# Turning 17 of 52 gathered fields on VectorE, with two marks and two pair blocks moved, in a DLRM tower on one core

## The reference

```
e = stack([tbl_f[ids[:, f]] for f in 26 fields])          # 512 x 26 x 128
sd = einsum('bfd,bd->bf', e, dense)
ss = einsum('bfd,bgd->bfg', e, e);  pairs = ss[:, iu, ju]  # 325 pairs
z = concatenate([dense, sd, pairs], 1);  h = concatenate([z, dense], 1)
h = maximum(h @ W_top1 + b_top1, 0)    # 607 -> 512
h = maximum(h @ W_top2 + b_top2, 0)    # 512 -> 256
y = h @ W_top3                         # 256 -> 1
```

## Time and profile before

| | us |
|---|---|
| median of 3 runs (lowest to highest) | 117.57 (117.4 to 118.24) |
| the profiled execution's own time | 117.33 |
| its span, first to last instruction | 115.3 |
| TensorE matmuls busy | 107.0 |
| VectorE busy | 62.2 |
| ScalarE busy | 62.1 |
| GpSimd busy | 58.3 |

### The profile page before, as it was taken

How to read it: one execution, slowest core, us unless ns; L and a number is a source line. 1 busy time by engine, 2 the same in 40 slices (tenths; PEclk the granted TensorE clock), 3 DMA queues, 4 the chain that set the end, 5 groups by cost and what they waited for, 6 DMA issues and landing times.

```text
span 115.3 us, 3393 instructions
## 1 busy us (share of the span) xinstructions
PE 107.0 (93%) x1514; PEld 86.8 (75%) x1514; DVE 62.2 (54%) x90; ACT 62.1 (54%) x82; POOL 58.3 (51%) x56
## 2 busy tenths in 40 slices
PE   5979899999999999999999998889999987999991
PEld 4637677868888888888887666768787875989891
DVE  0378998689897799798950007107131026008321
ACT  2379999993999999998930405003121016102220
POOL 0177788777777777788777506006677000000000
PEclk9999999999999999999999999999999999999999
DMA  1897976755766975999312201100212100000000
GB/s 41 248 299 276 287 281 227 244 137 200 275 179 218 347 205 144 374 276 336 84 46 51 67 1 28 28 6 23 50 47 68 28 6 0 6 0 6 6 0 1
DMA packets 6416, 14.84 MB, mean 129 GB/s; under 512 B 2125, under 2 KB 2637, under 8 KB 6402
## 3 DMA queue, kind: packets, MB, share of 16 engines
q1 hardware_dynamic: 4306, 10.94, 28.7%
q0 software_dynamic: 1664, 3.41, 10.7%
q10 hardware_dynamic: 432, 0.27, 0.8%
HBM read 14.62 MB, written 0.00 MB: 127 GB/s over the span
## 4 chain that ended last, share of the span: by engine, by line
PE 66%; ACT 13%; issue 9%; DVE 6%; DMA 4%; ACTq 1%
PE gram_ps L533 11%; PE h_ps L505 9%; PE h_ps L501 8%; PE gram_ps L501 7%; PE gram_ps L505 7%; ACT dist L294 5%; PE h_ps L557 5%; DMA raw<-oh 4%; PE h_ps L550 3%; PE h_ps L580 3%; ACT hi L282 3%; PE h_ps L567 3%; PE turn_ps L521 2%; ACT onehot L297 2%; DVE zfull L431 2%
## 5 line engine op out<-in xcount | busy, mean ns | idle before, releaser
L260 POOL DMA_INDIRECT got<-tbl,ids_sb x52 | 58.1, 1117 | 31.0 <-issue 14.9
L416 DVE TENSOR_SCALAR onehot<-ids_bc,rows_sb 128x1024 fp32r<-128x1024 int16 (+1 forms) x47 | 31.0, 718 | 5.4 <-DMA rows_sb<-rows 3.7
L418 DVE TENSOR_TENSOR lo<-raw,hi 128x1024 fp32r<-128x1024 f32 (+2 forms) x14 | 17.1, 1224 | 4.2 <-ACT hi L282 3.6
L501 PE MATMUL h_ps<-onehot,hi 128*128 128x512 f32 x60 | 16.7, 412 | 1.0 <-ACT onehot L297 0.8
L533 PE MATMUL gram_ps<-vecs 128*27 128x27 f32 x1024 | 13.3, 192 | 2.2 <-issue 1.5
L533 PEld LDWEIGHTS gram_ps<-vecs 128*27 128x27 f32 x1024 | 10.6, 104 | 6.3 <-issue 4.1
L308 ACT ACTIVATE vecs<-turn_ps 128x512 f32<-128x512 f32 (+2 forms) x16 | 8.2, 521 | 12.6 <-PE turn_ps L521 12.6
L505 PE MATMUL h_ps<-onehot,lo 128*128 128x512 f32 x60 | 15.0, 390 | 0.0
L501 PEld LDWEIGHTS h_ps<-onehot,hi 128*128 128x128 f32 x60 | 11.0, 192 | 5.1 <-ACT onehot L297 1.9
L431 DVE STREAM_TRANSPOSE zfull<-gram_ps 128x864 f32<-128x864 f32 x3 | 3.2, 1083 | 21.4 <-PE gram_ps L533 21.4
L297 ACT ACTIVATE onehot<-dist,rows_sb 128x1024 fp32r<-128x1024 f32 (+1 forms) x13 | 14.1, 1087 | 0.4
(11 more groups left out here) (55 smaller groups left out, 87.4 us busy)
## 6 DMA issues: line engine op xcount, KB each, us to landing
raw<-oh SPq DMA_DIRECT2D x8, 512.0 KB, 3.7
raw<-oh SPq DMA_DIRECT2D x4, 640.0 KB, 4.1
ids_bc<-ids_oh SPq DMA_DIRECT2D x6, 256.0 KB, 4.3
got<-tbl,ids_sb POOLq DMA_INDIRECT x52, 3.5
w1p_sb<-w_pairs SPq DMA_DIRECT2D x1, 702.0 KB
w1d_sb<-w_dense SPq DMA_DIRECT2D x1, 512.0 KB
w_sb<-w SPq DMA_DIRECT2D x1, 512.0 KB
raw<-oh ACTq DMA_DIRECT2D x2, 128.0 KB, 4.4
```

Source lines behind the costliest of these rows:

```text
L260: nc.gpsimd.indirect_dma_start(out=got[:, t, k, :], out_offset=None, in_=tables[k], in_offset=bass.IndirectOffsetOnAxis(ap=ids_sb[:, at:at ...
L416: nc.vector.tensor_scalar(there, row_numbers, rows_sb[:, c:c + 1], None, ALU.is_equal).then_inc(oh_dve, 1)
L418: nc.vector.tensor_tensor(lo[:, u % 2, 0:width(u)], raw[:, u % RAWS, 0:width(u)], hi[:, u % 2, 0:width(u)], ALU.subtract).then_inc(lo_read ...
L501: nc.tensor.matmul(banks[:, s, :], hi[:, u % 2, q * DIM:(q + 1) * DIM], onehot[:, u % 2, q * BATCH:(q + 1) * BATCH], start=(c == 0), stop= ...
```

## The change

Four edits, all of them of order and of which engine does what:

- Groups (2, 1), (2, 2), (2, 3), (3, 0) and (3, 1) are turned by VectorE. A group becomes 16 instructions of 32 partitions (a block of 32 samples by 32 dimensions for each field of the group), straight from `got` to `vecs`, with a semaphore on the last. TensorE's turns and ScalarE's moves of these groups go, and the banks of the others are counted anew (`BY_PE`). `gram` waits for both kinds. On VectorE the groups stand: (2, 1) and (2, 2) before the pair products of tile 0, (2, 3) between the zt copy of tile 0 and pair products 1, (3, 0) between the zt copy of tile 1 and `relu_h1b(0)`, (3, 1) between `relu_h2_far(0)` and pair products 2.
- In units 0 and 1 ScalarE marks nothing; VectorE marks all four columns.
- In TensorE's order the second and third pair blocks of tile 0 stand behind gram 1, the fourth behind the turn of the pairs of tile 1; one filler is added behind gram 0 in place of a turned group, and three go between gram 1 and layer 1 of tile 1.
- The last layer block takes its two banks in the other order.

```diff
+BY_DVE = [(2, 1), (2, 2), (2, 3), (3, 0), (3, 1)]
+BY_PE = [(t, i) for t in range(TILES) for i in range(GROUPS) if (t, i) not in BY_DVE]
+PE_GROUPS = [sum(u <= t for u, _ in BY_PE) for t in range(TILES)]
+DVE_GROUPS = [sum(u <= t for u, _ in BY_DVE) for t in range(TILES)]
...
-ACT_MARKS = [1, 1, 1, 1, 1, 1, 0, 1, 1, 1, 1, 1, 1, 1]
+ACT_MARKS = [0, 0, 1, 1, 1, 1, 0, 1, 1, 1, 1, 1, 1, 1]
...
-        banks_of = [h1_ps, h1_ps, turn_ps[1:3]]
+        banks_of = [h1_ps, h1_ps, [turn_ps[2], turn_ps[1]]]
...
             move_group(2, 0)
-            move_group(2, 1)
             near_pairs(0)
-            move_group(2, 2)
             near_pairs(1)
-            move_group(2, 3)
             relu_h1a(0)
             relu_h2(0)
-            move_group(3, 0)
             near_pairs(2)
-            move_group(3, 1)
             move_group(3, 2)
...
+            def turn_group(t, i):
+                dve.wait_ge(gathered[t][i], 16 * GROUP[i])
+                for r in range(QUADS):
+                    for c in range(QUADS):
+                        last = nc.vector.transpose(
+                            vecs[BLK * c:BLK * (c + 1), t * P + BLK * r:t * P + BLK * (r + 1),
+                                 GROUP_SLOT[i]:GROUP_SLOT[i] + GROUP[i]].rearrange("d b s -> d s b"),
+                            got[BLK * r:BLK * (r + 1), t, GROUP_AT[i]:GROUP_AT[i + 1], BLK * c:BLK * (c + 1)])
+                last.then_inc(dve_turned, 1)
...
+            turn_group(2, 1)
+            turn_group(2, 2)
             pair_products(0)
             zt_copy(0)
+            turn_group(2, 3)
             pair_products(1)
             zt_copy(1)
+            turn_group(3, 0)
             relu_h1b(0)
             relu_h2_far(0)
+            turn_group(3, 1)
             pair_products(2)
...
-                    pe.wait_ge(vecs_moved, GROUPS * t + GROUPS)
+                    pe.wait_ge(vecs_moved, PE_GROUPS[t])
+                    if DVE_GROUPS[t] > 0:
+                        pe.wait_ge(dve_turned, DVE_GROUPS[t])
...
             gram(0, 6, PARTS)
-            turn_group(2, 1)
             gram(0, 7, PARTS)
             layer1_dense(0, [3])
-            turn_group(2, 2)
-            keep_busy(2, 2 * GROUPS + 1)
+            keep_busy(2, PE_GROUPS[2])
+            keep_busy(2, PE_GROUPS[2])
...
             gram(1, 5, PARTS)
+            gram(1, 6, PARTS)
+            gram(1, 7, PARTS)
             layer1_pairs_of_tile(0, [1])
-            gram(1, 6, PARTS)
             layer1_pairs_of_tile(0, [2])
-            gram(1, 7, PARTS)
+            turn_pairs(1)
             layer1_pairs_of_tile(0, [3])
-            turn_group(2, 3)
-            keep_busy(0, 2 * GROUPS + 2)
-            keep_busy(0, 2 * GROUPS + 2)
-            turn_pairs(1)
-            keep_busy(0, 2 * GROUPS + 2)
             layer1_pairs_of_tile(1)
...
             gram(2, 7, PARTS)
-            turn_group(3, 0)
-            turn_group(3, 1)
             turn_group(3, 2)
+            turn_group(3, 3)
             turn_pairs(2)
-            turn_group(3, 3)
-            pe.wait_ge(vecs_moved, GROUPS * (TILES - 1) + 2)
             layer1_dense(2, [0])
```

More of the change, by code:

```diff
@@ L186, in dlrm_tower @@
         vecs_moved = sem("vecs_moved")
+        dve_turned = sem("dve_turned")
         gram_done = sem("gram_done")
@@ L306, in move_group @@
             def move_group(t, i):
-                act.wait_ge(turned, GROUPS * t + i + 1)
+                n = BY_PE.index((t, i))
+                act.wait_ge(turned, n + 1)
                 nc.scalar.activation(
                     vecs[:, t * P:(t + 1) * P, GROUP_SLOT[i]:GROUP_SLOT[i] + GROUP[i]],
-                    turn_ps[(GROUPS * t + i) % TURN_BANKS][:, 0:GROUP[i] * P].rearrange("d (s b) -> d b s", s=GROUP[i]),
+                    turn_ps[n % TURN_BANKS][:, 0:GROUP[i] * P].rearrange("d (s b) -> d b s", s=GROUP[i]),
                     ACT.Copy).then_inc(vecs_moved, 1)
@@ L515, in turn_group @@
             def turn_group(t, i):
-                n = GROUPS * t + i
+                n = BY_PE.index((t, i))
                 pe.wait_ge(gathered[t][i], 16 * GROUP[i])
```

## The result

The changed kernel took 125.06 us (median, 124.64 to 126.54), the kernel before 117.91: a ratio of 1.060, interval 1.053 to 1.067. It is 7.1 us slower, where 2.3 us faster was forecast. The profiled execution took 124.64, its span is 122.6 us.

What follows compares the result with a forecast made beforehand. TensorE was taken as the bound wherever fed. Gains of 1.1 and 0.59 us and the reorder, less VectorE's delays, ended layer 2 2.1 us earlier: 117.33 to 115.2, written 115.3; range 113.9 to 117.8.

Steps and rivals of the forecast that it cites:

- Head: Look-up part: moving two marks from ScalarE to VectorE starts everything behind it 1.1 us earlier, bounds 0 and 1.4.
- TensorE's turn of (2,1) off the path: Inside gram 0: the only moved turn that stood on the path, worth 0.59 us; gram 0 ends at 67.8.
- the price of a piece: Middle: time of one of VectorE's 16 small transposes per group, taken as 0.30, 0.27 or 0.24 us by size.
- the middle set, without overlap: VectorE's small transposes: 0.30, 0.27 and 0.24 us for 128, 96 and 64 elements, each waiting for the last.
- the four instructions of the chain: VectorE's first transposes of grams 0, 1 and 2 and the h1 half; before at 69.50, 78.36, 94.41 and 84.59 us.
- "Hidden" for (3,1): Before gram 2's end: VectorE's turn of (3,1) runs 86.4 to 91.2 and gram 2 ends at 92.3, costing nothing.
- VectorE becomes the bound of the middle: Rival: transposes dearer than 0.34 us delay VectorE's chain work, delays adding up; some 125 us at 0.44; chance 0.17.
- the pair copy's excess of 0.14 us: VectorE's pair copy takes 0.46 us, 0.14 over the fit; all of it added per transpose gives 0.44, 0.41, 0.38.
- its bounds: Transpose costs from 0.21, 0.18, 0.15 us (overlapped) up to 0.34, 0.31, 0.28, or 0.44, 0.41, 0.38 with all the excess.
- the case above it: Whole kernel: a time above 117.8 us, the start of the dear transposes, given some 0.17.
- The clock: Rival: TensorE's clock falls after fillers go and about 1 us idles behind gram 1; some 121 us; chance 0.04.
- Reorder of the pair blocks: TensorE at gram 1: two pair blocks of tile 0 move behind it, shortening its 7.13 us by 1.74.

Runs made afterwards that it cites:

- e1_head: The kernel before with only the marks of units 0 and 1 moved from ScalarE to VectorE; 123.39 us, ratio 0.995 (0.990 to 1.001).
- e4_one: The changed kernel with only group (2,1) on VectorE, the other groups back on TensorE and the bank swap undone; 115.17 us, no ratio.
- e8_fewer: The changed kernel with 9, 6 and 3 filler matmuls in TensorE's three holes, VectorE's work untouched; 122.57 us, ratio 1.043 to the kernel before.
- e9_two: The changed kernel with only groups (2,1) and (2,2) on VectorE, the three others on TensorE; 117.52 us, ratio 1.001 to the kernel before.
- e7_none: The changed kernel with no group on VectorE and the bank swap undone; 114.13 us, ratio 0.967 to the kernel before.
- e2_pairs: The kernel before with only TensorE's order changed between gram 1 and layer 1 of tile 1, three fillers out; 121.02 us, ratio 0.977.
- e10_one: The changed kernel with only group (2,1) on VectorE, bank swap undone, one more filler behind gram 0; 113.54 us, ratio 0.967 to the kernel before.

## Why the prediction was wrong

- Head: right, 1.0 of 1.1 us in the rows; the ratio of e1_head cannot tell it from nothing.
- TensorE's turn of (2,1) off the path: right for gram 0, which ends at 67.78 in e4_one as forecast; what it is worth in time is open.
- **The step that failed is the price of a piece.** "I take the middle set, without overlap": 0.30, 0.27, 0.24 us. The absence of overlap was right. The length was wrong: it was read from transposes that write densely, and the one argument on addresses ("the transposes read rows of 32 numbers that lie side by side") looked at what they read and not at what they write. They write in steps of 112 bytes and take 0.41, 0.35 and 0.29 us, at spacings of 0.426 (13.63 / 32), 0.36 and 0.30.
- The rest of the sum holds. Its own steps, done again with these spacings, put the four instructions of the chain at 71.7, 81.1, 89.1 and 99.4 us and the time at about 122.3 (an estimate); e8_fewer, in which the clock mostly stays up, has them at 71.81, 81.10, 89.01 and 99.64 and took 122.57.
- "Hidden" for (3,1) failed by the same price: at 0.42 us its pieces run 6.75 us from 93.79, and gram 2's transpose comes straight behind them at 100.57.
- The rival "VectorE becomes the bound of the middle" had the mechanism: each late group stands before an instruction of the chain. e9_two shows it for one group, the four late starts for all; that they simply add was not shown, since a part of (2,2)'s lateness is swallowed. Its number, "some 125" against 125.06, is luck. Its 0.44, 0.41 and 0.38 come from the pair copy's excess of 0.14 us, which no run explains, added in full to every size; they are too dear, by 0.08 us for the smallest, and the clock's 2 us are not in it. The two errors cancel.
- Between its bounds the forecast weighed a quarter of that excess for no measured reason, ended the range at 117.8 and gave the case above it 0.17. With 0.6 us for each 0.01 us of a piece, which the text had, an unmeasured price should have widened the range.
- The clock was a rival of its own at 0.04, for a hole of 1 us. It fell behind holes of 4.21, 3.21 and 1.86 us that the dear pieces made: the two were one case.
- Reorder of the pair blocks: right. The rows of e7_none have 1.7 us between gram 0 and gram 1 (1.5 expected), and the ratio of e2_pairs (2.3%, at least 1.3%) does not contradict them.

## What to carry to other kernels

Work moved to an idle engine is free only while it ends before that engine's next duty on the path: compare the pieces' total with the idle time in front of each duty. Here that is 13.6 us against 10.4, 5.8 against 3.6, 4.8 against 3.0 and 6.8 against 5.8, with the idle times of e7_none, which has the other edits. When many small instructions replace one, measure one of them in its exact form (addresses written, partitions changed) before pricing 80, and take the bad end of its bounds as seriously as the slope says. The two edits that needed no new instruction gave 3.3% by themselves.

## What was not expected of the hardware

- A write in steps of 112 bytes lengthens a VectorE transpose of 128 elements from 263 to 375 ns, but a plain copy to the same addresses from 207 to 259 only, and the pace within one quadrant only from 0.20 to 0.235 us. Why is open.
- TensorE has holes marked "issue" (nothing that the profile shows was waited for) in runs of small matmuls. In the profiles they sum to 1.5 us before, 3.3 in e4_one, 1.2 in e10_one (matmul records of the grams) and 0.3 in the changed kernel, where TensorE waits most. They are longer on the first chip (4.2 in e1_head, 3.0 in e2_pairs). Whether they move with the place of the instructions, with the chip or from execution to execution was not separated, and it was not tried what feeds them.
